# A graph network on one core: the last 32 rows of a split table packed into one block, and a fifth tile of the first layer fetched on TensorE

## The reference, cut to what matters

```python
h = relu(layernorm(x))
messages = h[src] * edge_probs[:, None] * weight             # first layer
out = segment_sum(messages, dst)
...
m = silu(einsum('ei,ej,ijh->eh', h[col], edge_attr, W_msg))  # second layer
...
msg = einsum('ei,eio->eo', h[src], W_rel[rel_type]) * e      # third, "relational"
...
w = kernel_net(edge_attr)                                    # fourth layer:
for i in range(4):                                           # four passes, same w
    msg = einsum('ei,eio->eo', nodes[src], w)
    nodes = gelu(segment_sum(msg, dst) / degree + nodes @ root_W[i] + root_b[i])
```

## Time and profile before

| | |
|---|---|
| median of three runs | 26634.41 us (26603.08 to 26652.0) |
| the profiled execution, its own time | 26617.11 us |
| its span, first to last instruction | 26615.3 us |
| TensorE busy | 20719.2 us, 78% of the span |
| VectorE (DVE) busy | 19332.0 us, 73% |
| ScalarE (ACT) busy | 13734.7 us, 52% |
| GpSimd (POOL) busy | 19283.0 us, 72% |
| TensorE's mean granted clock | 0.884 of full speed |

### The profile page before, as it was taken

The page is one execution under the profiler, slowest core; times in us unless marked ns, Lnnn a source line. Parts: engine busy times, 40 slices in busy tenths (PEclk is TensorE's granted clock), DMA queues, the critical chain, the costliest instruction groups (busy, mean ns, idle before and its releaser), DMA issues. The chain is left out here.

```text
span 26615.3 us, 414978 instructions
## 1 busy us (share of the span) xinstructions
PE 20719.2 (78%) x124290; PEld 13265.2 (50%) x124290; DVE 19332.0 (73%) x31590; ACT 13734.7 (52%) x14669; POOL 19283.0 (72%) x17673
## 2 busy tenths in 40 slices
PE   5777738888885888885888888588886888778886
PEld 2333326666653444443444444466664666556664
DVE  5555537777775777775777777688886888778886
ACT  4666601111112555553222222588886888778885
POOL 5777758888884666665777777677776777767776
PEclk9888968888887999997888888799997999889998
DMA  2222235555552222221333333466664666556664
GB/s 46 42 41 42 40 65 91 93 93 93 92 91 53 63 62 62 62 63 47 118 118 119 118 117 119 124 177 179 177 171 132 179 176 177 147 155 179 178 177 123
DMA packets 2209937, 2929.13 MB, mean 110 GB/s; under 512 B 979092, under 2 KB 1694178, under 8 KB 2182118
## 3 DMA queue, kind: packets, MB, share of 16 engines
q1 hardware_dynamic: 1250178, 2311.22, 29.5%
q0 software_dynamic: 814208, 166.54, 9.4%
q10 hardware_dynamic: 145440, 450.17, 4.4%
HBM read 2252.13 MB, written 674.06 MB: 110 GB/s over the span
## 5 line engine op out<-in xcount | busy, mean ns | idle before, releaser
L601 POOL DMA_INDIRECT got<-table,idx x14746 | 14929.0, 1012 | 6026.9 <-issue 4434.6
L778 PE MATMUL in_place<-place_hot,tparts 128*128 128x320 bf16 (+1 forms) x63408 | 11225.5, 338 | 2420.8 <-ACT place_hot L954 2420.7
L778 PEld LDWEIGHTS in_place<-place_hot,tparts 128*128 128x128 bf16 x63408 | 6449.6, 104 | 6568.0 <-ACT place_hot L954 2716.6
L949 ACT ACTIVATE near<-place_b,far_lanes 128x640 bf16<-128x640 f16 (+1 forms) x9180 | 6302.8, 771 | 216.8 <-DMA place_b<-place_row 216.3
L1087 DVE TENSOR_REDUCE msg<-prod 128x64 f32<-128x1024 f32 x4040 | 4906.8, 1215 | 103.3
L954 ACT ACTIVATE place_hot<-near,one 128x5760 bf16<-128x5760 bf16 (+1 forms) x1020 | 4805.9, 4712 | 33.2
L1454 POOL DMA_INDIRECT added<-add_rows,add_idx x2222 | 3690.9, 1661 | 766.2 <-issue 617.6
L1079 DVE TENSOR_TENSOR prod<-w_in,got 128x1024 f32<-128x1024 f32 x2424 | 2913.4, 1222 | 695.8 <-DMA got<-table,idx 580.6
L939 ACT ACTIVATE outb<-run 128x256 f32<-128x256 f32 (+1 forms) x1010 | 737.6, 730 | 4124.9 <-DVEq L1124 4124.9
L1497 PE MATMUL acc<-hot,spread 128*128 128x392 bf16 x12120 | 2399.1, 352 | 0.0
L890 ACT ACTIVATE h<-h1p,b 128x512 f32<-128x512 f32 x808 | 544.3, 686 | 2682.5 <-DVE wcopy L1072 2544.4
(11 more groups left out here) (253 smaller groups left out, 17587.0 us busy)
## 6 DMA issues: line engine op xcount, KB each, us to landing
w_in<-kept SPq DMA_DIRECT2D x2424, 512.0 KB, 3.3
kept<-wcopy ACTq DMA_DIRECT2D x808, 512.0 KB, 2.7
got<-table,idx POOLq DMA_INDIRECT x14746
attr<-in_edge_attr SPq DMA_DIRECT2D x202, 1024.0 KB
rows<-in_src_row SPq DMA_DIRECT2D x202, 704.0 KB
sums<-outb SPq DMA_DIRECT2D x1010, 128.0 KB
place_b<-place_row SPq DMA_DIRECT2D x612, 160.0 KB
range_b<-range_row SPq DMA_DIRECT2D x609, 160.0 KB
```

What stands on the lines that cost most here:

```text
L601: pool.indirect_dma_start(out=dst[:, j * width:(j + 1) * width], out_offset=None, in_=table, in_offset=bass.IndirectOffsetOnAxis(ap=idx[:, ...
L778: mm = pe.matmul(in_place[b][:, h, :], tparts[:, s, t, :], place_hot[:, b, t, h * XC:(h + 1) * XC], start=(t == 0 and s == 0), stop=(t == ...
L949: act.activation(near[:, t, :], place_b[:, b, :], ACT.Abs, bias=SB["far_lanes"][:, t:t + 1]).then_inc(S["near_made"], 1)
```

## The change

In the first layer X becomes 5: 11 tiles of a chunk are gathered and 5 fetched on TensorE, in two halves of 320 columns.

In every fetch on TensorE, the last block of the table takes its three pieces at once. `table_parts` loads the last 32 rows three times, onto partitions 0-31, 32-63 and 64-95, cuts them as before, and then copies the second piece of the second 32 partitions and the third piece of the third into the block of the first piece. The lanes of that block name the same 32 places three times (and -1 on the last 32 partitions), so one product sums all three pieces: 12 x 3 + 1 = 37 products for 39. SP issues the 12 full loads without waiting for the cleared block, and 15 loads in place of 13.

```diff
+LAST = RANGE - (KT - 1) * P
...
+                for t in range(KT - 1):
+                    sp.dma_start(whole[:, t, :].rearrange("r (o f) -> r o f", o=OWNERS), v[t * P:(t + 1) * P, :, :]).then_inc(loaded, 16)
+
                 sp.wait_ge(zeroed, 1)
-                for t in range(KT):
-                    w = min(P, RANGE - t * P)
-                    sp.dma_start(whole[0:w, t, :].rearrange("r (o f) -> r o f", o=OWNERS), v[t * P:t * P + w, :, :]).then_inc(loaded, 16)
+                for s in range(PIECES):
+                    sp.dma_start(whole[s * LAST:(s + 1) * LAST, KT - 1, :].rearrange("r (o f) -> r o f", o=OWNERS), v[(KT - 1) * P:RANGE, :, :]).then_inc(loaded, 16)
...
-                dve.wait_ge(loaded, 16 * KT)
+                dve.wait_ge(loaded, 16 * (KT - 1 + PIECES))
...
+                for s in range(1, PIECES):
+                    r = slice(s * LAST, (s + 1) * LAST)
+                    c.step(dve.tensor_copy(parts[r, 0, KT - 1, :], parts[r, s, KT - 1, :]))
...
-    X = {"weighted": 4, "relational": 4, "kernel_net": 0, "kernel_kept": 5}[kind]
+    X = {"weighted": 5, "relational": 4, "kernel_net": 0, "kernel_kept": 5}[kind]
...
-                        for s in range(PIECES):
+                        for s in range(PIECES if t < KT - 1 else 1):
                             for h in range(XH):
                                 mm = pe.matmul(in_place[b][:, h, :], tparts[:, s, t, :], place_hot[:, b, t, h * XC:(h + 1) * XC],
-                                               start=(t == 0 and s == 0), stop=(t == KT - 1 and s == PIECES - 1))
+                                               start=(t == 0 and s == 0), stop=(t == KT - 1))
...
+    def lanes():
+        rows = np.arange(P)[:, None] + P * np.arange(KT)[None, :]
+        rows[:, KT - 1] = np.where(np.arange(P) < PIECES * LAST, (KT - 1) * P + np.arange(P) % LAST, -1)
+        return rows.astype(np.float32)
...
-        "const_lanes": (np.arange(P)[:, None] + P * np.arange(KT)[None, :]).astype(np.float32),
-        "const_far_lanes": -(np.arange(P)[:, None] + P * np.arange(KT)[None, :]).astype(np.float32),
+        "const_lanes": lanes(),
+        "const_far_lanes": -lanes(),
```

## The result

The changed kernel takes 26255.9 us, the median of 4 runs (26245.07 to 26260.89); the kernel before took 26627.75 us beside it (4 runs, 26603.08 to 26652.0). The ratio is 0.986, with a 95% interval of 0.9843 to 0.9877. The forecast was 26307 us, in a range from 26240 to 26440. The gain is 372 us where 327 was forecast.

A forecast was written before the change was run, and what follows sets the result against it. GpSimd's gathers bound the first layer and kept passes; in the relational layer DVE and TensorE wait for each other. -252 - 83 + 8 = -327 us gave 26290, plus 17 for the median: 26307 us, range 26240 to 26440.

The forecast's parts named there:

- Term 1: First layer: 11 gathers a chunk for 12, 1.25 us less in each of 202 chunks, 252 us gained.
- The low end, 90 us: First layer: gain if gathers took the kept passes' mean of 1052 ns, making the chunk 14.9 us.
- Term 2: First layer: no other engine needs more than the new 14.11 us chunk; TensorE nearest, slack 0.5 to 1.6 us; cost nothing.
- 0.5 us by the kept passes' rate: First layer: TensorE's slack a chunk if its products partly run at 1.2 GHz, 13.6 us needed of 14.11.
- Term 3: Relational layer: two products fewer cut the wait of DVE's fourth product by 0.41 us a chunk, 83 us gained.
- Term 4: Kept passes: TensorE saves 0.55 us a chunk behind GpSimd's 14.9 us, so gain 0; stages unchanged to 0.3%.
- The forecast's price without the cover, 334 us: Kept passes: gain if GpSimd's pace did not hide TensorE's saved 0.55 us a chunk; as a rival, 25973 us, chance 0.03.
- Term 5: Table loading, five times: 1.7 us more each, 8 us in all; bounds 0 (three short loads cost one) and 15.
- that rival: Relational layer gives nothing, since a moving pause of TensorE's clock can cost 0.4 us a chunk; 26390 us, chance 0.12.
- no new bound: Denies the rival that TensorE or ScalarE binds the first layer at 14.7 us a chunk; 26427 us, chance 0.09.
- the gathers did not stretch: Denies the rival that longer gathers keep the first layer's chunk at 15.3 us; 26559 us, chance 0.04.
- the slower case: First layer: TensorE stays at 1.2 GHz, 22.8 us a chunk, whole time about 28,050 us; chance 0.03.

The follow-up runs named there:

- the filled pause: Changed kernel plus 14 products of zeros behind the last quarter of every second relational-layer chunk; 33940.67 us, 1.0154 of the kernel before, on a slower chip.

## Why the forecast held, and where it was off

**The sum.** Two of its terms carry the result, and both stood at the place and with the mechanism that the forecast gave. -252 measured -260.7, and with the block taken away the kernel kept it. -83 measured -108.7, and with the block taken away it was gone. The two were 34 us short, and the rest added 3 us: -14.3 and +19.4 for a forecast +8. Those last two are differences between two executions, of a size that other pairs of executions show too.

**Term 1, a gather less.** The count, the issue gap (676.8 / 2222 = 0.305 us) and the issue-only idle time came as forecast. The step that was off is that the excess of the long gathers "stays whole". It was 12 x 0.031 = 0.37 us and is 11 x 0.030 = 0.33, which is 0.04 of the 0.043 us a chunk by which the term was short. Taken over the layer, it is the gathers beside the message product that shortened, from 1.20 to 1.16 us in the mean; those beside the scan went only from 1.03 to 1.02, so the 1.00 us in the timeline, for 1.08 before, is not the rule. Part of it is spread: on the other chip this layer's gathers take 975 to 977 ns in the same 2222, and 2841.5 to 2846.4 us for 2840.1, a gain of 254 to 259 us. The low end, 90 us, with the kept passes' gathers, was rightly left. The gather beside the widened one-hots took 0.94 us, so the 14 us that the forecast estimated by the Trainium skill (SBUF — State Buffer, "Who interferes with whom") did not come; no row stood behind its 0.02 us a gather either. The section's rule that an instruction of DVE with two inputs in SBUF contends with GpSimd's reads agrees with the gathers of 1.21 and 1.00 us.

**Term 2, nothing else binds.** Right, and the slack was at least what was claimed: 12 more products left GpSimd's pace as it was. The forecast's 0.5 us by the kept passes' rate was the wrong one of its two values. TensorE's wait for one-hots fell to a half, not to a third. That fits what the forecast named for its clock, at a granted 0.97 it does its products faster and so pauses for longer than the kept passes' rate gave, but no run tests this by itself.

**Term 3, the relational layer.** The wait of 0.56 us became 0.15, as worked out: 84.6 us over the 202 fourth products, for 83. Two more products out changed nothing, which shows that this wait was used up at 0.15. What was short is the step that let everything behind simply move along. The other 24 us stand at the first two products of a turn, behind the pause (-37.0 and +14.4 us), and at nothing else but 1 us. There the first matrices run at the slow pace in 53 turns and not in 98, and from the end of the pick to the first product it is 3.2 us in the mean and not 3.5. The forecast had this, "a little more if fewer matrices run at 1.2 GHz", as its upper bound, without a price. It comes with the block: the kernel without it has 98 such turns, and the two other kernels with it on that chip have 58 and 59. Its course is read from the rows, the slow products now falling into the quarter ahead of the pause; the filled pause, made to test it, ran only where TensorE had another bound.

**Term 4, the kept passes.** 0 was right to 0.5% (-4.0, -10.8 and +0.5 us in 3010), not to the 0.3% said: the second pass moved 0.36%. It was the kernel before that had a long one there, 3016.1 us, and other traces have such a pass too (3018.2 us in the kernel with two more products out). The forecast's price without the cover, 334 us, did not come.

**Term 5, the load.** All five loads together are 2.1 us longer, 4 us between executions on one chip, and not 8. Three short loads together cost what two long ones took, 1.57 us for 2 x 0.77, and the two copies 0.20 each as forecast. The term lies nearer to its lower bound.

**The rivals.** The relational layer gave more than nothing: the pause did move, as that rival said, but the other way. The first layer has no new bound; the gathers did not stretch; the kept passes did not gain; and TensorE's clock rose in the first layer, where the slower case had it fall. On the two chips of the longer time the change is on the slower side, as its two nearest variants show. That comes at the place that the forecast named for it, TensorE's products in the first layer, but more by gaps of issue than by the lower clock.

## What to carry to other kernels

Price a removed piece of work by the wait behind it, down to the gap that the waiting engine's own previous step leaves, and stop there: the first two products gave 0.41 us a chunk there and the next two nothing. Where an engine pauses, look also at what runs behind the pause: fewer slow matrices there gave another 24 us. Where one engine's idle time is issue time alone, its count of instructions is the stage, and the others can take more work as long as nothing that it needs comes late. When two engines wait for each other, look for a small operand that is made late between them: the one-hot of 0.75 us, made half a chunk earlier, brought 478 us, more than the change itself, and on the changed kernel.

## What the runs showed of the hardware

- The same program took 26,650 us on one chip and 33,421 and 33,389 us on two others, in nearly all of its executions, and on the latter TensorE's products in the first layer come one by one in stretches, with 0.82 to 0.84 us of idle time before each in the mean. There the change itself would be slower than the kernel before, to judge by the two variants that differ from it only in the relational layer (1.015 both), where on the chip of the comparison it is faster.
- Work on TensorE can shorten its own neighbours: with 12 empty products a chunk the granted clock of the first layer rose from 0.97 to 1.00 and the real products went from 306 to 299 ns. With 78 products for 74 and none empty it is the same 1.00 and 299 ns.
- After a pause of 4.13 us the 12 matrices took 2.74 us, and 1.48 us otherwise, in the relational layer; with the pause gone the granted clock of this stage is 0.97 and not 0.92.
- Where the slow products fall can matter more than how many there are. With the block the quarter ahead of the pause went from 2.2 to 3.0 us in the mean and the matrices behind it from 2.7 to 2.2 us. The stage's granted clock went from 0.93 to 0.92, and the stage became shorter.
- A gather that GpSimd issues takes 0.94 us alone, 1.16 to 1.20 us in the mean beside DVE's product of two operands in SBUF, and 0.95 us beside its one-hots with one.
